# SwiGLU of each row tile moved into the steps of the last head pair, and scores for the own batch alone

## What is computed

```python
def _L1_xattn_ref(query, key, value, mask, wq, wk, wv, wo, curr_seq_pos):
    ...
    q = _apply_rope(q, curr_seq_pos)
    k = _apply_rope(k, curr_seq_pos)
    raw = jnp.einsum('bhqd,bhkd->bhqk', q, k) / scale
    attn = jax.nn.softmax(masked, axis=-1)
    out = jnp.einsum('bhqk,bhkd->bhqd', attn, v)
    return out @ wo

def _L1_ffn_ref(x, w_gate, s_wgate, w_up, s_wup, w_down, s_wdown, inv_gate, inv_up, inv_inter):
    x_flat = x.reshape(-1, H).astype(jnp.bfloat16)
    qg, sg = _dynamic_quant(x_flat, inv_gate)
    qu, su = _dynamic_quant(x_flat, inv_up)
    gate_out = _quant_gemm(qg, sg, w_gate, s_wgate)
    up_out = _quant_gemm(qu, su, w_up, s_wup)
    inter = jax.nn.silu(gate_out) * up_out
    inter = jnp.clip(inter, -SWIGLU_LIMIT, SWIGLU_LIMIT).astype(jnp.bfloat16)
    qi, si = _dynamic_quant(inter, inv_inter)
    out = _quant_gemm(qi, si, w_down, s_wdown)

x = x + jnp.tanh(g_xattn[1]) * _L1_xattn_ref(_layernorm(x, axis=-1), ctx_4096, ctx_4096, ...)
x = x + jnp.tanh(g_ffn[1]) * _L1_ffn_ref(_layernorm(x, axis=-1), ...)
```

## Time and profile before

| what | us |
|---|---|
| median of 3 runs | 888.03 (887.2 to 889.19) |
| the profiled execution's own time | 889.1 |
| its span in the profile | 887.3 |
| granted TensorE clock, mean | 0.958 of full |
| PE busy | 789.7 (89%) |
| DVE busy | 674.1 (76%) |
| POOL busy | 364.9 (41%) |
| ACT busy | 353.1 (40%) |

### The profile page before, as it was taken

The page is one execution under the profiler, slowest core; times in us unless marked ns, Lnnn a source line. Parts: engine busy times, 40 slices in busy tenths (PEclk is TensorE's granted clock), DMA queues, the critical chain, the costliest instruction groups (busy, mean ns, idle before and its releaser), DMA issues. The chain is left out here.

```text
span 887.3 us, 13314 instructions
## 1 busy us (share of the span) xinstructions
PE 789.7 (89%) x4276; PEld 621.9 (70%) x4276; DVE 674.1 (76%) x1250; ACT 353.1 (40%) x1063; POOL 364.9 (41%) x300
## 2 busy tenths in 40 slices
PE   2899987978799999979999988999999999993774
PEld 2565554867688788868778867887887887772663
DVE  5798897878787877748877765877775878776994
ACT  2777775222233433324343322433332333242642
POOL 2687777224542532314343322433431423103562
PEclk9899999988899999999999999999999999997887
DMA  8210030100110211001121010111100102002001
GB/s 266 80 48 24 24 100 1 37 24 24 48 49 24 60 40 33 26 24 38 34 60 36 24 37 13 48 48 36 48 24 24 48 13 54 1 1 71 13 35 48
DMA packets 37443, 37.46 MB, mean 42 GB/s; under 512 B 2896, under 2 KB 27216, under 8 KB 37392
## 3 DMA queue, kind: packets, MB, share of 16 engines
q1 hardware_dynamic: 35168, 32.81, 12.6%
q10 hardware_dynamic: 2224, 3.94, 1.4%
HBM read 34.64 MB, written 2.10 MB: 41 GB/s over the span
## 5 line engine op out<-in xcount | busy, mean ns | idle before, releaser
L922 POOL TENSOR_TENSOR dense<-rope_a,rope_b 128x512 f32<-128x512 f32 x62 | 79.6, 1284 | 224.2 <-DVE rope_b L1037 224.2
L967 ACT ACTIVATE e_sb<-masked,nmax 128x64 f32<-128x64 f32 x256 | 86.0, 337 | 86.0 <-DVE nmax L1066 85.7
L976 ACT ACTIVATE ot_hi<-PB 128x512 fp32r<-128x512 f32 x64 | 38.4, 599 | 194.1 <-PE PB L1282 194.1
L1198 PE MATMUL QB<-xT_hi,wq_lo 128*128 128x512 f32 x256 | 109.2, 426 | 2.4 <-DVE xT_lo L1110 2.4
L1198 PE MATMUL ROW<-wo_hi,ot_lo 128*128 128x512 f32 x256 | 102.6, 401 | 7.6 <-DVE ot_lo L1084 6.8
L1199 PE MATMUL QB<-xT_lo,wq_hi 128*128 128x512 f32 x256 | 103.5, 404 | 0.0
L1200 PE MATMUL QB<-xT_hi,wq_hi 128*128 128x512 f32 x256 | 103.4, 404 | 0.0
L1199 PE MATMUL ROW<-wo_lo,ot_hi 128*128 128x512 f32 x256 | 101.6, 397 | 0.0
L1200 PE MATMUL ROW<-wo_hi,ot_hi 128*128 128x512 f32 x256 | 101.1, 395 | 0.0
L1034 DVE TENSOR_TENSOR rope_a<-QB,rope 128x512 f32<-128x512 f32 x62 | 42.9, 691 | 75.9 <-PE QB L1200 75.2
L1037 DVE TENSOR_TENSOR rope_b<-QB,rope 64x512 f32<-64x512 f32 x124 | 85.4, 689 | 3.9
(11 more groups left out here) (202 smaller groups left out, 1914.9 us busy)
## 6 DMA issues: line engine op xcount, KB each, us to landing
raw<-in_wq SPq DMA_DIRECT2D x32, 256.0 KB, 2.7
raw<-in_wo SPq DMA_DIRECT2D x32, 256.0 KB, 2.6
ctx_two<-in_ctx SPq DMA_DIRECT2D x16, 256.0 KB, 3.8
x_sb<-in_x SPq DMA_DIRECT2D x8, 256.0 KB, 7.5
ctx_raw<-in_ctxT ACTq DMA_DIRECT2D x1, 2048.0 KB, 11.7
raw<-in_wv SPq DMA_DIRECT2D x8, 256.0 KB, 2.8
raw<-in_wk SPq DMA_DIRECT2D x8, 256.0 KB, 2.9
out<-x_sb SPq DMA_DIRECT2D x8, 256.0 KB, 2.0
```

What stands on the lines that cost most here:

```text
L922: nc.gpsimd.tensor_tensor(dst, a, b, ALU.add).then_inc(s_rot, 1)
L967: nc.scalar.activation(e_sb[:, r, :], masked[:, r, :], ACT.Exp, bias=nmax[:, r:r + 1], accum_out=zsum[:, r:r + 1]).then_inc(s_exp, 1)
L1198: nc.tensor.matmul(out, lhs[1], rhs[0], start=first, stop=False)
```

## The change

The two blocks of layer 1 become one, `attention_and_swiglu`. The first three pairs run as before, but for `score`. The last pair gets a list of its own on every engine (`last`), of 22 steps n: tile t has its mean and variance in step 10 + t (STATS), which is the step where its last output product is added, and its SwiGLU stages in steps 11 + t (SMOOTH), 12 + t (GATE), 13 + t (INTER) and 14 + t (DOWN). Where a stage stands in a step, `ffn_tile(n, stage)` gives its tile.

```diff
+        STATS, SMOOTH, GATE, INTER, DOWN = range(10, 15)
+        STEPS = DOWN + TILES
+            def last():
+                for n in range(STEPS):
...
+                    if (t := ffn_tile(n, INTER)) is not None:
+                        inner_scales(t)
+                    if (t := ffn_tile(n, SMOOTH)) is not None:
+                        scales(t)
+                    if 1 <= n < SLOTS:
+                        normalize(N, n)
+                    if (t := ffn_tile(n, GATE)) is not None:
+                        inner(t)
+                    if (t := ffn_tile(n, DOWN)) is not None:
+                        add_down(t)
+                    if 2 <= n <= SLOTS + 1:
+                        accumulate(N - 2, (n - 2) % 8)
+                    if (t := ffn_tile(n, STATS)) is not None:
+                        stats(t)
+                    if 1 <= n <= SLOTS:
+                        rest_ot(N - 1)
+                    if (t := ffn_tile(n, STATS)) is not None:
+                        to_bf16(t)
```

That is DVE's list. On POOL, with both clips now there and no longer on DVE:

```diff
+            def clip(t):
+                pool.wait_ge(s_qm, 2 * t + 2)
+                nc.gpsimd.tensor_scalar(xs[t % 2], xs[t % 2], ROUND + QMAX, ROUND - QMAX, ALU.min, ALU.max)\
+                  .then_inc(s_clip, 1)
...
+                    if n in (8, 9):
+                        fold_gate_up(n - 8)
+                    if n == 10:
+                        for i in range(2):
+                            weight_rest(i, wgu[1][i], wgu_raw[i], wgu[0][i])
+                    if (t := ffn_tile(n, INTER)) is not None:
+                        inner_clip(t)
+                    if (t := ffn_tile(n, GATE)) is not None:
+                        inner_smooth(t)
+                    if (t := ffn_tile(n, SMOOTH)) is not None:
+                        clip(t)
+                    if (t := ffn_tile(n, STATS)) is not None:
+                        inverse_deviation(nc, pool, c, s_var, s_rstd, t, t + 1, 3 + t)
+                    if n == 11:
+                        for k in range(IC):
+                            fold_down(k)
+                    if n == 12:
+                        for k in range(IC):
+                            weight_rest(2 + k, wd[1][k], wd_raw[k], wd[0][k])
```

`smooth(t)` stands at the head of POOL's step, before `rotate`. On ACT a step is: `round_pt`, `exps`, `inner_quantise`, `gate` (Tanh in place of Silu, straight from PSUM), `quantise`, `round_ot`, `inner_to_stationary`, `to_stationary`. On PE:

```diff
+                    if n < SLOTS:
+                        if (t := ffn_tile(n, DOWN)) is not None:
+                            down(t)
+                        if (t := ffn_tile(n, GATE)) is not None:
+                            gate_up(t)
+                    if 2 <= n <= SLOTS + 1:
+                        outputs(LAST, N - 2, n - 2)
+                    if 1 <= n <= SLOTS:
+                        if n in (DOWN, DOWN + 1):
+                            pe.wait_ge(s_x, n - DOWN + 1)
+                        weighted(LAST, N - 1, n - 1)
...
+                    if (t := ffn_tile(n, INTER)) is not None:
+                        inner_transposes(t)
+                    if (t := ffn_tile(n, SMOOTH)) is not None:
+                        q_transposes(t)
```

```diff
-                out = SB_[:, :].rearrange("p (kb r k) -> p kb r k", kb=2, r=4)
...
                         q = q_rot[:, unit % 2, 2 * i + b, 2 * r:2 * r + 2, :].rearrange("p h s -> p (h s)")
-                        mm = nc.tensor.matmul(out[:, :, 2 * b + r, :], q,
-                                              keys.rearrange("p (kb k) -> p kb k", kb=2), start=True, stop=True)
+                        a = 2 * b + r
+                        mm = nc.tensor.matmul(SB_[:, S * a:S * a + S], q, keys[:, S * b:S * b + S],
+                                              start=True, stop=True)
```

More of the change, by code:

```diff
@@ L862, in grouped_attention @@
         c = c | {"wo": wo}
+        magic = sb("magic", [P, 1])
+        xb = sb("xb", [P, D], BF16)
+        ib = sb("ib", [P, INNER], BF16)
+        am, sc, rs = (sb(n, [P, 2, 2]) for n in ("am", "sc", "rs"))
+        sc_gu, sci = sb("sc_gu", [P, 2]), sb("sci", [P, 2])
+        ami, rsi = sb("ami", [P, 1]), sb("rsi", [P, 1])
+        s_wgu, s_wd, s_fold = sem("wgu_loaded"), sem("wd_loaded"), sem("factors_folded")
+        s_fhi, s_flo = sem("ffn_w_hi_ready"), sem("ffn_w_lo_ready")
+        s_magic, s_xb, s_xs = sem("magic_ready"), sem("xb_ready"), sem("xs_ready")
@@ L864, in grouped_attention, with down_bank, ffn_tile @@
+        th = rope_a[:, 0:INNER]
+        prod = rope_a[:, INNER:2 * INNER]
+        xi = [rope_b[:, INNER * p:INNER * p + INNER] for p in range(2)]
+        TQ, GU, TI = QB, KV, TB
+        LAST = PAIRS - 1
+        STATS, SMOOTH, GATE, INTER, DOWN = range(10, 15)
+        STEPS = DOWN + TILES
+        def down_bank(t):
+            return PB2[:, 0, :] if t + DOWN < SLOTS else SB_[:, :]
+        def ffn_tile(n, stage):
+            return n - stage if 0 <= n - stage < TILES else None
         TX = [SB_, TB, QB[1], OB, SB_, TB, OB, SB_]
@@ L958, in _ @@
+            with pool.Fori(0, LAST) as gp:
                 pair(gp, True)
-            pair(PAIRS - 1, False)
-            inverse_deviation(nc, pool, c, s_var, s_rstd, 0, TILES - 1, 3)
+            last()
         @block.scalar
@@ L1018, in pair, with quantise, to_stationary @@
                 round_ot(SLOTS * gp + SLOTS - 1)
-            with act.Fori(0, PAIRS - 1) as gp:
+            def quantise(t):
+                act.wait_ge(s_rs, t + 1)
+                act.wait_ge(s_magic, 1)
+                p = t % 2
+                for n in range(2):
+                    nc.scalar.activation(xs[p][:, n, :], xs[p][:, n, :], ACT.Identity, bias=magic[:, 0:1],
+                                         scale=rs[:, p, n:n + 1]).then_inc(s_qm, 1)
+            def to_stationary(t):
+                act.wait_ge(s_ft, t + 1)
+                if t:
+                    act.wait_ge(s_gu, t)
+                for n in range(2):
+                    nc.scalar.activation(q_t[:, n, :, :], TQ[n][:, :].rearrange("p (k t) -> p k t", k=KC),
+                                         ACT.Copy, bias=-ROUND).then_inc(s_qt, 1)
@@ new lines, in gate, with inner_quantise @@
+            def gate(t):
+                act.wait_ge(s_gu, t + 1)
+                if t:
+                    act.wait_ge(s_prod, t)
+                else:
+                    act.wait_ge(s_rot, q_job(LAST, 11) + 1)
+                nc.scalar.activation(th, GU[:, 0:INNER], ACT.Tanh, scale=sc[:, t % 2, 0:1]).then_inc(s_th, 1)
+            def inner_quantise(t):
+                act.wait_ge(s_rsi, t + 1)
+                nc.scalar.activation(xi[t % 2], xi[t % 2], ACT.Identity, bias=magic[:, 0:1],
+                                     scale=rsi[:, 0:1]).then_inc(s_qi, 1)
@@ L1021, in _ @@
+            with act.Fori(0, LAST) as gp:
                 pair(gp, True)
-            pair(PAIRS - 1, False)
+            last()
         @block.vector
@@ L1167, in pair @@
                         rest_ot(N - 1)
-                    if n >= 11 and not ahead:
-                        final_rows(n - 11)
                     if n in K_SLOTS and (n != 13 or ahead):
@@ L1179, in pair, with stats @@
                 rest_ot(N - 1)
-                if not ahead:
-                    for tile in range(5, 7):
-                        final_rows(tile)
-                    dve.wait_ge(s_mv, 2 * TILES - 1)
-                    variance_eps(nc, c, s_var, 0, TILES - 1)
-                accumulate(N - 1, 7)
-            with dve.Fori(0, PAIRS - 1) as gp:
+                accumulate(N - 1, 7)
+            def stats(t):
+                final_rows(t)
+                dve.wait_ge(s_mv, TILES + t + 1)
+                variance_eps(nc, c, s_var, t, t + 1)
@@ L1188, in _ @@
+            with dve.Fori(0, LAST) as gp:
                 pair(gp, True)
-            pair(PAIRS - 1, False)
-            final_rows(TILES - 1)
-            dve.wait_ge(s_mv, 2 * TILES)
-            variance_eps(nc, c, s_var, TILES - 1, TILES)
+            last()
         @block.tensor
@@ L1640, in gate_up @@
                         for h in (1, 0):
[L1641 to L1642 removed]
+                            mm = nc.tensor.matmul(GU[:, n * INNER:(n + 1) * INNER], q_t[:, n, k, :],
+                                                  wgu[h][n][:, k, :], start=(k == 0 and h == 1),
                                                   stop=(k == KC - 1 and h == 0))
[L1644 removed]
+                mm.then_inc(s_gu, 1)
@@ L1674, in rope_tables @@
+            with pe.Fori(0, LAST) as gp:
+                pair(gp, True)
+            last()
 def rope_tables(scale):
```

511 lines of the change are left out of this document (239 added, 272 removed).

## The result

| what | before | after |
|---|---|---|
| median, us | 888.6 (4 runs) | 878.7 (4 runs) |
| ratio, 95% interval | | 0.986 (0.983 to 0.990) |
| last write of x in the profiled execution | 884.7 | 874.95 |
| xb of tile 0 written | by 810.3 | 776.7 |

The change is faster by 1.4% (1.0 to 1.7%). I had forecast 877.3 and 874.0 for the last write of x. Two kernels further down, `best1_fill` and `best2`, each had one execution that ran far longer (2595 and 1909 us); their ratios leave it out, and without it their medians would be 0.7 and 0.2 lower.

A forecast was written before the change was run, and what follows sets the result against it. It saw PE and DVE busiest in late attention and SwiGLU, POOL idle through attention's end. Overlapped: first xb 777.3, steps near 10.3, last tile 22.7, x complete at 874.0, not 884.7; 888.0 - 10.7 = 877.3 us, range 864 to 889.

The forecast's parts named there:

- the clip: POOL's clip of 1024 columns in each SwiGLU step: 2.08 us taken, between ends of 1.04 and 2.25.
- my estimate of 0.9: POOL's clip by the Trainium skill's near line rate: 0.9 us, a step of 9.1, the whole some 9 us less.
- The chain leads narrowly; what is late next is DVE: In a full overlapped step the chain takes 10.3 us, DVE's own load 9.1, perhaps 10.1 with p_sb beside POOL.
- my sum: Last pair: first xb at 777.3, steps of 10.3 with delays, last tile 22.7; x complete at 874.0 instead of 884.7.
- The second rival: Late overlapped steps: PE becomes the bound and the kernel slower, deciding from a clock of some 0.84; 890.5 us at 0.70; chance 0.13.
- The scores: Halved score columns in every attention step: 128-column weight loads set the pace of 0.111 us, so a gain of 0.
- The estimate of 14 us: Scores of 58 steps: if loads took the skill's 81 ns, halving columns would give 14 us.
- The first tile: Steps 10 and 11 of the last pair: xb of tile 0 done at 777.3, after POOL's low parts and inverse deviation.
- The delays by `fold_down` and wd's low parts: POOL's one-time work delays tiles 2 and 3: 1.7 us each on top of a step of 10.3.
- What would show it: Signs: xb writes 10 to 12 us apart, clip near 2.1, score loads 0.11 apart, clock above 0.84, first pairs unchanged.
- my mark of a wrong mechanism: In the overlapped steps: xb writes following each other faster than 9 us would mean the mechanism is wrong.
- the 25 us of the rival: Third rival: score columns set the pace, 25 us more gained over 58 steps, 852 in all; chance 0.12.

The follow-up runs named there:

- best1_fill: Kernel of best1 plus 24 unread fp32r products on PE in three waits of its last three steps: 871.3 us, ratio 0.980 against the kernel before.
- best2: Changed kernel with the edits of gate_first and pool_gaps and the unread products of best1_fill, DVE's down addition in its old place: 868.1 us, ratio 0.9745.
- clip_twice: Changed kernel with POOL's clip of 1024 columns done twice and PE's transposes waiting for the second: 883.7 us, ratio 0.994 against the kernel before.
- gate_first: Changed kernel with down and gate and up ahead of the output and weighted products on PE in all steps: 871.4 us, ratio 0.979.
- pool_gaps: Changed kernel with POOL's one-time weight work moved into its gaps and tile 0's inverse deviation ahead of the low parts: 872.7 us, ratio 0.981.
- best1: Changed kernel with gate_first and pool_gaps together, and DVE's down addition behind the accumulation and statistics: 875.1 us, ratio 0.983.
- before_own_scores: Kernel before the change with only the own batch's 64 keys in the scores, nothing else changed: 887.6 us, ratio 0.9973.
- swiglu_behind: Changed kernel with SwiGLU's five stages six steps later, so that it no longer overlaps the scores: 901.7 us, ratio 1.013 against the kernel before.

## Why the prediction was right, and where it was not

**The total** (877.3 against 878.7) is right by two errors of 8 to 9 us that cancel.

**Too high: the clip.** The step that failed is "the nearest is a product in place by a single column, 1.04 for 512, so 2.08 for 1024". I scaled a two-input operation by its elements. A one-input operation takes 1.04 for 1024. Eight clips are 8.3 in the sum; a second clip in each step cost 7.5 us in the stretch (`clip_twice`), changes of the clock included. The Trainium skill, GPSIMD Engine Reference, § 4.1, has one-input operations there at about line rate; the trace agrees, and my estimate of 0.9 from it was nearer than the row that I preferred.

**Too low: PE.** "The chain leads narrowly; what is late next is DVE" failed. What is late next is PE. Against my sum with a clip of 1.04 the distances to tiles 2, 4, 6 and 7 are 0.7, 2.1, 2.9 and 3.1 longer and the last tile 1.0. First, gate and up stand behind the output products from step 16 on (`gate_first`: 5.5 of the 6.0 in the distances to tiles 6 and 7). Second, in step 14 the clock is low just after PE has waited for POOL's clip, and the scores and the mask are late with it: `pool_gaps`, with the same lists in that step and a clock of 1.00, has 1.6 less there. No run moves the clock of that step by itself, so that it was the clock stays argued, and why it fell stays open. Third, the last tile runs at 0.65 (`best1_fill`: 4.1 with the order of `best1`). My sum had the last tile at 22.7 with gate and up alone at the low clock, and it took 22.66, again with a clip one too long and PE pieces too short.

The second rival named PE, as a sum of busy times with a clock of 0.84 as the point of decision, which I gave 0.13. As a mean over the seven distances the sum stayed below the step (56.1 of 75.6, clock 0.88). In two of them it did not: to tile 4 PE is busy 11.38 of 11.40 at 0.85, to tile 2 11.04 of 11.66 at 0.76, and there the rival was nearly right. To tiles 6 and 7 PE is busy 8.0 of 11.6 and 8.3 of 11.8 and was on the path all the same, by its order. A mean of an engine's work does not tell whether a step waits for it.

**The scores**: a gain of 0 forecast, 0.04 a step measured, 2.4 us (0.7 to 4.1) in the kernel before. The reason given, the loads, holds: with 16, 64 and 128 columns eight loads take the same 0.97, with 64 weight columns 0.54. The estimate of 14 us by the 81 ns of the Trainium skill, TensorE: Matmul & The Clock Gate, § Back-to-back issue gap, is not borne out for these fp32 products.

**The first tile**: 776.7 against 777.3, by the chain that I wrote (POOL's low parts, then the inverse deviation, DVE waiting 4.0 for it). **The delays by `fold_down` and wd's low parts**, 1.7 each in the sum: without them the distances lose 0.9 and 2.0 (`pool_gaps`).

**What would show it**: the mask of step 11 late, yes; the xb writes 10 to 12 apart, two of seven not (8.7 and 9.5, beside 10.9 to 11.8; less than 9 was my mark of a wrong mechanism, and it marks the clip); clip near 2.1, no; clock above 0.84 as a whole (0.88), but 0.83 in the stretch from 786.4 to 798.1. DVE waits for PE's scores in two of the five late steps, 12 and 14 (1.5 and 1.9), not in most. The first three pairs as long as before, no: from the first mask to that of the last pair 444.1 in place of 445.2, and 443.3 in `before_own_scores`, which is 48 steps of 0.04. By my own words that is a sign of a wrong mechanism; it is small beside the 25 us of the rival.

## What to carry to other kernels

Where a step is one loop through four engines, follow each engine's list for the instruction that the loop waits for, and ask what stands ahead of it: an order that hides PE's work in one group of steps can put it on the path in the next. A one-input operation isn't priced by a two-input one. Look at PE's busy time step by step, for the mean hides the steps that it fills. If the last stretch of a kernel is a chain with PE waiting in it, try unread products in those waits: 24 of them gave 4 us here.

## What the hardware showed that I had not expected

Fewer moving columns save next to nothing (0.04 us a step of eight loads) while the weights keep 128 columns in plain fp32: eight loads take 0.97 us with 16, 64 or 128 columns, and 0.54 with 64 weight columns. PE's pieces at the low clock take 1.6 to 1.8 times as long as at the full one, not twice: eight transposes 1.97 against 1.11, four down products 2.09 against 1.21, gate and up 3.43 against 2.19; in `gate_first` the single products of this last piece go from 0.41 to 0.28 half way, so a piece can straddle both levels.

Some of DVE's instructions stay in work until the POOL instruction that they meet is over, whatever their own size. Xb takes 1.48 in place of 0.55 beside a two-input POOL operation of 512 columns (tiles 1 and 2), and 2.62 beside one of 1024 (tile 0 in `pool_gaps`, 770.04), and ends 0.28 behind it each time; there sc, of two columns, takes 1.18 in place of 0.17. The normalised probabilities p_sb take 1.40 in place of 0.42 in 55 of their 64 executions, each beside a POOL operation. Other instructions do not mind: the masks meet a POOL operation in 60 of 64 cases and always take 0.41 to 0.43, and the scale of the inner row, sci, of one column, keeps its 0.15.

And with SwiGLU in the softmax's steps PE's granted clock is higher: 0.88 with PE busy 56 of 75.6 us between the first and the last xb, where `swiglu_behind` has 0.67 with 42 of 69.8. The part behind the softmax has a share in it (0.93 from 824.0 to 852.3).
